# First slots of a gated cross-attention block: who sums, who scales, and in which order the ternary weights are built

## The reference

```
q = rms_norm(linear(layernorm(x), q_w, q_b), norm_q_w)
k = rms_norm(linear(ctx, k_img_w, k_img_b), norm_k_img_w)
v = linear(ctx, v_img_w, v_img_b)
x = x + tanh(g_xattn) * linear(softmax(q k' / sqrt(32)) v, o_w, o_b)

wg    = bf16(w).reshape(-1, 64)                 # groups of 64 weights
scale = clip(mean(|wg|), 1e-8)
w_t   = clip(round(wg / scale), -1, 1) * scale  # for W_fc (2048x512) and W_proj (512x2048)
h = relu(layernorm(x) @ W_fc_t') ** 2
x = x + tanh(g_ffn) * (h * rsqrt(mean(h*h) + eps)) @ W_proj_t'
```

## Time and profile before

| | us |
|---|---|
| median of 3 runs | 1010.25 (1009.19 to 1010.44) |
| the profiled execution | 1009.37 |
| its span in the trace | 1007.6 |
| TensorE busy | 930.6 (92%) |
| VectorE busy | 690.1 (68%) |
| ScalarE busy | 717.9 (71%) |
| GpSimd busy | 566.1 (56%) |

### The profile page before, as it was taken

The page is one execution under the profiler, slowest core; times in us unless marked ns, Lnnn a source line. Parts: engine busy times, 40 slices in busy tenths (PEclk is TensorE's granted clock), DMA queues, the critical chain, the costliest instruction groups (busy, mean ns, idle before and its releaser), DMA issues.

```text
span 1007.6 us, 26077 instructions
## 1 busy us (share of the span) xinstructions
PE 930.6 (92%) x9942; PEld 570.9 (57%) x10043; DVE 690.1 (68%) x1360; ACT 717.9 (71%) x1235; POOL 566.1 (56%) x616
## 2 busy tenths in 40 slices
PE   4776597899999999999999999999999999999997
PEld 1343354566665656666666565666666665656663
DVE  7898987777677677767767676767677776766200
ACT  2777767678777777777877777777787777777653
POOL 1223334665656565767656565657666566656655
PEclk9797798999999999999999999999999999999999
DMA  8735431333333344343323334433343423232200
GB/s 302 182 82 149 107 91 43 75 75 75 74 71 68 75 85 86 85 75 75 81 69 75 70 72 80 86 85 75 78 81 68 79 69 72 55 64 54 43 21 21
DMA packets 184588, 82.43 MB, mean 82 GB/s; under 512 B 170000, under 2 KB 170000, under 8 KB 182928
## 3 DMA queue, kind: packets, MB, share of 16 engines
q1 hardware_dynamic: 184464, 80.77, 36.1%
HBM read 30.67 MB, written 8.39 MB: 39 GB/s over the span
## 4 chain that ended last, share of the span: by engine, by line
PE 78%; issue 7%; ACT 4%; DVE 3%; POOL 2%; DVEq 0%; POOLq 0%; ACTq 0%
PE mix_ps L440 10%; PE up_pair L426 10%; PE up_pair L427 9%; PE mix_ps L439 8%; PE score_ps L397 7%; PE score_ps L396 7%; PE score_ps L395 7%; PE tr_a L395 2%; PE tr_a L397 2%; PE tr_a L396 2%; PE score_ps L510 2%; PE score_ps L487 2%; PE mix_ps L577 1%; PE tr_a L440 1%; PE up_pair L449 1%
## 5 line engine op out<-in xcount | busy, mean ns | idle before, releaser
L426 PE MATMUL up_pair<-ft,w 128*128 128x256 f16 x960 | 217.1, 274 | 1.2 <-ACT h_sb L791 1.2
L427 PE MATMUL up_pair<-ft,w 128*128 128x256 f16 x960 | 217.1, 275 | 0.0
L440 PE MATMUL mix_ps<-w,big 128*128 128x512 bf16 x464 | 176.1, 380 | 10.0 <-issue 8.6
L1628 POOL TENSOR_TENSOR k_weighted<-k_raw,qk_norm 128x512 f32<-128x512 f32 x32 | 41.9, 1310 | 253.6 <-DVE k_raw L1157 252.1
L1642 POOL TENSOR_TENSOR big<-h_sb,big 128x512 f16<-128x512 f32 x128 | 155.0, 1211 | 14.8 <-ACT big L797 8.7
L1652 POOL TENSOR_TENSOR hh_sum<-hh_sum,hh_sb 128x512 f32<-128x512 f32 x112 | 154.3, 1378 | 4.9 <-ACT hh_sb L813 4.9
L439 PE MATMUL mix_ps<-w,big 128*128 128x512 bf16 x382 | 145.1, 380 | 2.9 <-POOL big L1642 2.9
L862 ACT ACTIVATE score_ps<-score_ps,log_p,exp_scale 128x512 f32<-128x512 f32 x128 | 95.7, 748 | 58.7 <-PE score_ps L513 58.7
L1069 DVE TENSOR_TENSOR p_lo<-score_ps,p_hi 128x512 f16<-128x512 f32 x128 | 88.1, 689 | 47.4 <-ACT p_hi L744 47.0
L791 ACT ACTIVATE h_sb<-up_pair,relu_scale 128x512 f32<-128x512 f32 x120 | 81.3, 678 | 36.9 <-PE up_pair L427 36.3
L426 PEld LDWEIGHTS up_pair<-ft,w 128*128 128x128 bf16 x960 | 94.4, 98 | 19.4 <-ACT h_sb L791 1.9
...
## 6 DMA issues: line engine op xcount, KB each, us to landing
...
```

What stands on the lines that cost most here:

```text
L426: nc.tensor.matmul(dst[:, half], w, ft[i][:, c, :], start=(c == 0), stop=False)
L427: last = nc.tensor.matmul(dst[:, half], w, ft[i][:, C + c, :], start=False, stop=(c == C - 1))
L440: last = nc.tensor.matmul(dst[:, :], ht_lo[i][:, row], w2[:, m, :], start=False, stop=(m == M - 1))
```

## The change

- **Setup.** The bounds of the q and v weights come from `weight_sum` on ScalarE (a sum of absolute values, with another constant in `w_step`); `weight_max` on VectorE is left for the k weights alone.
- **Context.** The bound of context tiles 2 to 6 is a sum too, by ScalarE (`context_total`, tile `ctx_sum`), put behind `q_hi` in slots 0 to 2 and behind the second `relu` in slots 3 and 4. The other tiles keep VectorE's `context_max`.
- **Small row operations.** VectorE's two operations behind `bn_aggr` are gone: GpSimd's `norm_rows` adds and scales the variance itself and subtracts the mean. VectorE's `k_unscale` and `o_unscale` are replaced by one GpSimd operation on two columns (`unscales`), for which `k_out` and `x1_out` wait. This holds in every slot.
- **Halves.** In slots 3 and 4 ScalarE copies each half out of PSUM (`raw_half`), and VectorE clips the pair once in SBUF. The products of pair 12 and the work on pairs 13 to 15 move later; pair 15 is masked and multiplied in slot 5, around `tops_t`.
- **TensorE.** A half of a group sum waits for ScalarE's copies (`raw_ready`) instead of VectorE's clips (`tscale_ready`). `warm` before `tops_t` is 6 instead of 10 (slots 1, 2) or 12 (slots 3, 4); 8 and 6 are added around the last group sums of slots 1 and 2.

```
             def ternary_half(n):
                 pe.wait_ge(abs_ready, n // 2 + 1)
-                pe.wait_ge(tscale_ready, n)
+                pe.wait_ge(raw_ready, n - HALVES)
                 group_sum(n, up_b)
...
             def early_slot(t):                      # TensorE
-                warm(10)
+                warm(6)
                 tops_t(t)
...
                 ternary_pair(p + 2)
+                warm(8)
                 ternary_pair(p + 3)
+                warm(6)
             def middle_slot(t):
-                n = 2 * HALVES + 6 * (t - 3)
+                n = 2 * HALVES + 4 * (t - 3)
                 ternary_half(n)
-                warm(12)
+                warm(6)
...
+            def raw_half(n):                        # ScalarE
+                p = n // 2
+                act.wait_ge(gsum_done, n + 1)
+                need(act, tsigned_ready, p - TD + 1)
+                copy_hi(t_scale[p % TD][:, n % 2 * 512:(n % 2 + 1) * 512], up_b, raw_ready)
+            def context_total(t, par):
+                act.wait_ge(ctx_in[par], 16 * (t // 2 + 1))
+                act.wait_ge(ctx_spread, t)
+                act.wait_ge(qss_ready, t)
+                nc.scalar.activation(square_out[:, :], ctx_sb[par][:, :], ACT.Abs, accum_out=ctx_sum[:, :]).then_inc(ctx_part_ready, 1)
...
             def row_stats(src, raw, mv, done, n):   # VectorE
                 nc.vector.bn_stats(raw[:, :], src).then_inc(done, 1)
                 nc.vector.bn_aggr(mv[:, :], raw[:, :]).then_inc(done, 1)
-                nc.vector.tensor_scalar(pair[:, 0:1], mv[:, 0:1], -1.0, None, ALU.mult).then_inc(done, 1)
-                nc.vector.tensor_scalar(pair[:, 1:2], mv[:, 1:2], LN_EPS, X_SCALE ** -2, ALU.add,
-                                        ALU.mult).then_inc(done, 1)
...
-            def ternary_half(n):
-                dve.wait_ge(gsum_done, n + 1)
-                nc.vector.tensor_scalar(t_scale[p % TD][:, n % 2 * 512:(n % 2 + 1) * 512], up_b, TERNARY_CLIP, None,
-                                        ALU.max).then_inc(tscale_ready, 1)
...
+            def unscales(t):                        # GpSimd
+                pool.wait_ge(ctx_step_ready, t + 1)
+                nc.gpsimd.tensor_tensor(unscale[t % 3][:, :], ctx_step[:, :].to_broadcast([P, 2]), unit_scale[:, :],
+                                        ALU.mult).then_inc(unscale_ready, 1)
```

More of the change, by code:

```diff
@@ L1029, in closing_slot @@
                 squares(g, j, 3)
+            weight_sum(0)
             for s in range(3):
+                if s == 2:
+                    weight_sum(2)
                 weight_hi(s)
@@ L1687, in slot @@
                 if more:
+                    unscales(t + 1)
                     k_weight(t + 1)
```

178 lines of the change are left out of this document (93 added, 85 removed).

## The result

| | before | changed |
|---|---|---|
| median (range, runs) | 1009.72 (1007.72 to 1010.44, 4) | 1035.83 (1033.37 to 1038.37, 4) |
| the profiled execution | 1009.37 | 1033.37 |
| its span | 1007.6 | 1031.6 |

What follows compares the result with a forecast made beforehand. TensorE was taken to bound 277 to 950 us, VectorE slots 0 to 2, so gains only in the first 195 us. Setup -1.65 and slots -5.6 give -7.25: 1002.1, plus 0.88, forecast 1003.0 us, range 998.5 to 1008.0.

Steps and rivals of the forecast that it cites:

- Small row operations: Slots 0 and 1: moving VectorE's one-column operations to GpSimd, with shorter dead matmuls in slot 1, gains 0.6 us together.
- The 27 later slots: Slots after slot 5: bound by TensorE, GpSimd's additions hidden in its wait for k rows; 0, bound +0.1 a slot.
- Rival E: Slower: GpSimd's added 0.8 us a slot reaches TensorE through k rows or second norm; about 1016.5 us, chance 0.05.
- Setup, -1.65: Ahead of slot 0: ScalarE's v bound and a cheaper q bound bring the first `scores` 1.65 us sooner, all arriving.
- Slots 0 to 2: Shift without the setup: -0.6 us at the start of slot 2's tops, -1.25 at their transpose, -1.85 after it.
- Slots 2 and 3: Fewer dead matmuls and earlier tops take the shift without the setup from -1.85 us in slot 2 to -3.2.
- the large term: Slot 3 to 4: reordered ternary work, summed over ScalarE, gains 4.67 us, less 0.8 for half clock; shift -7.05.
- Slot 4 to 5 and pair 15: Slot 5's tops gain nothing more; pair 15's late products delay TensorE's `scores_t`, +1.45 us, leaving a shift of -5.6.
- Rival B: Slots 2 to 4: fewer dead matmuls ahead of `scores_t` leave TensorE at half clock, about 3.3 us; 1006.3, chance 0.09.

Runs made afterwards that it cites:

- e1: The changed kernel, with GpSimd negating the mean by one more one-column operation and adding it in the row norm: 1011.62 us, ratio 1.0009.
- f3: The kernel before, with only the bounds of the q and v weights as ScalarE sums: 1009.34 us, ratio 0.9985.
- e4: The changed kernel with row statistics and row norm as before (VectorE makes both columns, GpSimd adds); GpSimd keeps `unscales`: 1006.49 us, ratio 0.9971.
- f1: e4 with slot 5's down blocks 14 and 15, which need ternary pair 15, issued behind `scores_t`: 1005.65 us, ratio 0.9963.
- h1: g4 with 20 more filler matmuls ahead of the tops' transpose of slot 4: 1005.10 us, ratio 0.9938.
- g4: f1 with 20 filler matmuls that nobody reads, where TensorE waits in slots 4 and 5: 1006.11 us, ratio 0.9945.
- h2: e1 with pair 15's blocks moved as in f1, the 20 fillers of g4 and the 20 more of h1: 1006.24 us, ratio 0.9955.
- g2: f2 with 20 filler matmuls in slots 4 and 5 and pair 15's blocks moved as in f1: 1006.80 us, ratio 0.9949.
- f2: e4 with VectorE's `k_unscale` and `o_unscale` back, so no small operation is moved to GpSimd: 1013.19 us, ratio 1.0021.
- e3: The kernel before with 36 GpSimd operations appended behind all other work: at 512 columns, two-scalar forms with a subtract took 2.08 us, add and multiply 0.77.
- e2: The kernel before, with only GpSimd's row norm changed to subtract the mean instead of adding minus the mean: 1028.71 us, ratio 1.0181.

## Why the prediction was wrong

**The step that failed** is in "Small row operations": "GpSimd takes them over with one operation of 0.19, started as soon as the means are there, so its own chain does not get shorter or longer." I costed the operation that was added and not the one whose form changed with it. The text ahead of the prediction names the norm (L1600) among GpSimd's lines and says that GpSimd "subtracts the mean", and I carried the norm's 0.8 over unseen. It measured 2.1, twice a slot. No row of the trace of before had a scalar subtract on GpSimd of any length, so this price should have been bounded, not taken as known.

**The 27 later slots**, taken at 0 with a bound of +0.1, came out at +0.72 each. Per slot GpSimd's busy time went from 17.4 us (420.4 in 673/27.9 slots) to 21.2: 2 x 1.29 for the form, 2 x 0.34 for `ln_in`, 0.22 for `unscales`, 3.5 x 0.155 for slower sums (1378 to 1533 ns), less 2 x 0.13 for a quicker `ln_rstd`, 3.75 in all (means over the whole run; a slower q step and quicker low parts, 0.18 each, cancel). I had 0.84 and a slack of 6.8. The slack was read at the wrong wait: what stands behind the k rows had 2.4, and what stands behind the second norm's wait had none of it. Of the 3.75, 3.5 stand behind the k rows, and 1.5 of them behind that wait in the slots that grew by 1.56. e1 bounds what is harmless: its GpSimd has 1.8 us a slot more than before (464.9 us busy in the same stretch), and its steady slots are no longer than before (27.83 and 27.88 us).

**Rival E** had the path, GpSimd reaching TensorE by its second norm, but with 0.8 us of added work a slot and a chance of 0.05. Its own break-even, 0.27 a slot, was right to look for; the question "what if one of these operations is dearer than the nearest row" was not asked.

**Setup, -1.65.** Right. First `scores` at 36.83 (37.1 predicted); f3 alone gives -1.5 in time, and all of it arrives.

**Slots 0 to 2.** With the small operations on GpSimd the step was wrong in sign. From slot 0 to slot 2 the table has e1 lose 1.1 us where e4 gains 0.5, and the changed kernel lose 3.1. In slot 1, ScalarE's chain to the tops of slot 2 waits for GpSimd's `xn`. Before, and changed:

```profile
87.40 0.87 POOL L1597 TENSOR_TENSOR ln_rstd<-ln_in,minus_half 128x1 f32<-128x1 f32 x1 [3.03 <-issue]
88.46 1.30 POOL L1600 TENSOR_SCALAR xn<-x_sb,ln_in,ln_rstd 128x512 f32<-128x512 f32 x1 [0.18 <-POOL ln_rstd L1597]
...
89.79 0.63 ACT L744 ACTIVATE x_rows<-xn 128x512 f16<-128x512 f32 x1 [3.29 <-POOL xn L1600]
```

```profile
87.79 0.49 POOL L1609 TENSOR_SCALAR ln_in<-ln_mv 128x1 f32<-128x1 f32 x1 [1.52 <-issue]
88.36 0.89 POOL L1611 TENSOR_TENSOR ln_rstd<-ln_in,minus_half 128x1 f32<-128x1 f32 x1
89.35 2.19 POOL L1613 TENSOR_SCALAR xn<-x_sb,ln_mv,ln_rstd 128x512 f32<-128x512 f32 x1
...
91.58 0.63 ACT L748 ACTIVATE x_rows<-xn 128x512 f16<-128x512 f32 x1 [3.14 <-POOL xn L1613]
```

From GpSimd's first step to the end of the norm it was 2.4 us and is 3.75: 0.5 for the small operation, 0.9 for the pass. That chain has no cover, since ScalarE waits 3 us for it either way.

**Slots 2 and 3 and the large term.** The prediction counts by the transposes (L498), which stood 1.2 to 1.5 us behind the step of the table in these slots. With VectorE's statistics (e4) they stand at 93.99 (slot 2), 123.14 (slot 3) and 155.66 (slot 4), where 94.7, 123.9 and 155.5 were predicted; in the changed kernel at 98.33, 128.86 and 162.72. So the sum over ScalarE's chain held up to there: in e4 3.8 us gained from slot 3 to slot 4 where 4.67 were named, the rest having come earlier.

**Slot 4 to 5 and pair 15**, +1.45 predicted. The wait was there and as long as computed (1.40), at the place named. But it cost 2.7 (f1 against e4, 30.60 to 27.93), since the clock fell behind it: that step's size was wrong, a stall of TensorE priced at its length, without the half-pace work behind it. Another 1.7 was lost ahead of it: e4's tops of slot 5 start at 187.44, where 185.75 was predicted. Part of it is the lower clock behind the tops of slot 4: without it the way to the tops of slot 5 takes 33.43 in place of 35.25 in two later versions (h1 against g4), 1.8 us where 0.8 was set aside.

**Rival B**, the clock, was put at 3.3 us, because of fewer dead matmuls ahead of `scores_t`. In sum it was worth about that where VectorE makes the statistics (h1 against e4, 0.9938 to 0.9971, with pair 15), and 5 to 7 in versions whose timing let it fall more often (h2 against e1, g2 against f2, both with pair 15). That it came out near 3.3 is luck in part: the rival had the clock lost behind the shorter runs ahead of `scores_t` in slots 2 to 4, and more of it was lost behind the waits of slots 4 and 5. The Trainium skill, TensorE: Matmul & The Clock Gate, "What's actually happening", has it that activity releases the throttle; the fillers' 1.00 in place of 0.64 agrees.

**What is open.** Why one version of two with the same 2.4 us wait keeps the clock is not settled; what TensorE did in the microseconds ahead of the wait is nearly equal in both. Why GpSimd is slower with a subtract is not known; that it is, e3 shows. Where the last 1 to 2 us between h1 and h2 lie was read from traces and not tried by itself, and so was the path from the long norm to TensorE; e2 and e1 show its price. The changed kernel as it is, with fillers, was not run.
